# Storing the latents' z once as float32 and cutting it into high and low parts in the perceiver

## The reference, cut to what matters

```python
# z: what the perceiver's queries, keys and values are computed from, per batch
z_x   = layernorm(layernorm(x))  * ln_l_g + ln_l_b     # 512 rows, 512 features
z_ctx = layernorm(ctx)           * ln_x_g + ln_x_b     # 77 rows, 512 features
q     = z_x @ Wq                                       # 16 heads of 64
k, v  = concat(z_ctx, z_x) @ Wkv                      # the kernel keeps z_x first, then z_ctx
out   = softmax(q k^T / 8, masked) v
```

## Time and profile before

| what | value |
|---|---|
| median of 3 runs | 3122.73 us (3119.6 to 3123.52) |
| the profiled execution | 3116.59 us |
| its span, first to last instruction | 3114.8 us |
| PE busy | 2756.6 us, 88% |
| DVE busy | 2101.4 us, 67% |
| ACT busy | 1575.4 us, 51% |
| POOL busy | 1466.0 us, 47% |
| latents stage, by the trace | 923 to 1049 us |
| perceiver stage, by the trace | 1049 to about 2640 us |

### The profile page before, as it was taken

How to read it: one execution, slowest core, us unless ns; L and a number is a source line. 1 busy time by engine, 2 the same in 40 slices (tenths; PEclk the granted TensorE clock), 3 DMA queues, 4 the chain that set the end, 5 groups by cost and what they waited for, 6 DMA issues and landing times. The chain is left out here.

```text
span 3114.8 us, 43373 instructions
## 1 busy us (share of the span) xinstructions
PE 2756.6 (88%) x15650; PEld 2323.5 (75%) x15650; DVE 2101.4 (67%) x4249; ACT 1575.4 (51%) x3064; POOL 1466.0 (47%) x1087
## 2 busy tenths in 40 slices
PE   6788889986868499999999999999999998689687
PEld 5677777765434389898898988989889897577476
DVE  4766666661338577777777877777777777457655
ACT  2333333321104467676776767767677676101175
POOL 2454444331001155555555555556555565356555
PEclk9899999996975699999999999999999999789899
DMA  5111111114018732323223232233322311857474
GB/s 180 50 49 53 53 53 53 39 35 169 1 50 323 282 70 69 97 70 111 66 69 97 76 105 66 69 100 79 99 68 67 97 51 44 290 203 242 176 263 169
DMA packets 184000, 335.11 MB, mean 108 GB/s; under 512 B 52008, under 2 KB 58155, under 8 KB 176749
## 3 DMA queue, kind: packets, MB, share of 16 engines
q1 hardware_dynamic: 161553, 257.30, 27.9%
q0 software_dynamic: 11680, 45.02, 3.9%
q10 hardware_dynamic: 10560, 30.08, 2.5%
HBM read 164.30 MB, written 146.61 MB: 100 GB/s over the span
## 5 line engine op out<-in xcount | busy, mean ns | idle before, releaser
L1671 POOL TENSOR_SCALAR pa_Pr<-pa_Pr,pa_rs 128x590 f32<-128x590 f32 x512 | 904.1, 1770 | 671.9 <-DVE pa_rs L1898 671.8
L1902 DVE TENSOR_REDUCE pa_least<-pa_S 128x1 f32<-128x590 f32 x512 | 390.5, 763 | 186.3 <-PE pa_S L1735 184.3
L1827 ACT ACTIVATE pa_Pr<-pa_S,pa_least 128x590 f32<-128x590 f32 x512 | 385.8, 753 | 110.0 <-DVE pa_least L1902 105.3
L1852 DVE TENSOR_TENSOR pa_PTl<-pa_W,pa_PTh 128x512 fp32r<-128x512 f32 (+1 forms) x640 | 414.9, 681 | 11.1 <-ACT pa_PTh L1796 8.0
L1796 ACT ACTIVATE pa_PTh<-pa_W 128x512 fp32r<-128x512 f32 (+1 forms) x640 | 366.8, 596 | 96.4 <-PE pa_W L1746 82.2
L1746 PE MATMUL pa_W<-pa_ident,pa_Pr 128*128 128x128 f32 (+1 forms) x2560 | 367.5, 274 | 7.2 <-DVE pa_PTl L1852 5.8
L1746 PEld LDWEIGHTS pa_W<-pa_ident,pa_Pr 128*128 128x128 f32 (+1 forms) x2560 | 302.2, 142 | 37.4 <-DVE pa_PTl L1852 11.8
L1760 PE MATMUL pa_O<-pa_PTh,pa_V 128*128 128x512 f32 (+1 forms) x640 | 288.6, 451 | 16.2 <-DVE pa_PTl L1852 12.2
L1761 PE MATMUL pa_O<-pa_PTl,pa_V 128*128 128x512 f32 (+1 forms) x640 | 252.5, 394 | 0.0
L1733 PE MATMUL pa_S<-pa_U,pa_Qh 128*128 128x296 f32 (+1 forms) x1024 | 228.0, 304 | 7.7 <-DMA pa_Um<-pa_U 7.4
L1735 PE MATMUL pa_S<-pa_Um,pa_Ql 128*128 128x296 f32 (+1 forms) x1024 | 223.4, 300 | 0.0
(11 more groups left out here) (470 smaller groups left out, 6808.1 us busy)
## 6 DMA issues: line engine op xcount, KB each, us to landing
xs_s<-pa_Ql SPq DMA_DIRECT2D x57, 576.0 KB
pa_Um<-pa_U SPq DMA_DIRECT2D x128, 147.5 KB
pa_Qh<-pa_Qh SPq DMA_DIRECT2D x128, 128.0 KB
o_s<-pa_O_hi SPq DMA_DIRECT2D x64, 256.0 KB, 2.0
o_s<-pa_O_lo SPq DMA_DIRECT2D x64, 256.0 KB, 2.3
ex_o_hi<-o_s SPq DMA_DIRECT2D x7, 2048.0 KB, 11.0
ex_o_lo<-o_s SPq DMA_DIRECT2D x7, 2048.0 KB, 16.1
z_s<-la_z_hi ACTq DMA_DIRECT2D x8, 1180.0 KB, 7.3
```

What stands on the lines that cost most here:

```text
L1671: pool.tensor_scalar(p, p, rs[:, g % 2, t:t + 1], None, ALU.mult).then_inc(*pool_s.mark("probs", n))
L1827: act.activation(Pr[g % 2][:, t, :], scored[n % 2], ACT.Exp, scale=-1.0, bias=least[:, g % 2, t:t + 1], accum_out=rs[:, g % 2, t:t + 1]).t ...
L1852: dve.tensor_tensor(out, src, f32(hi_ap), ALU.subtract).then_inc(*dve_s.mark(*name))
L1902: dve.tensor_reduce(least[:, g % 2, t:t + 1], scored[n % 2], AX, ALU.min).then_inc(*dve_s.mark("least", n))
```

## The change

z is stored once, as float32, and cut after it is loaded. In the latents, L1419, L1421, L1474 and L1423 and the tiles z_hi and z_lo go; `full` is stored by one transfer. In the perceiver, `load(b)` brings one transfer of 1180 KB into z[1]. ScalarE copies each chunk of it into z[0] (the high part), and VectorE replaces the chunk in z[1] by its difference from z[0] (the low part). For batch 0 this stands between the cuts of weights 1 and 2. For a later batch chunks 0 and 1 are cut in tick 64b-9 and chunks 2 and 3 in tick 64b-8: on ScalarE behind the exponential of the tick and ahead of its copies of transposes, on VectorE at the end of the tick. The first query product waits chunk by chunk for the low part. As z[1] is now written by the load while z[0] is written later, `load(b)` waits for the old batch's last key and last value product.

```diff
 build_latents, scalar:
-                    act.wait_ge(*dve_s.before(i, "lo", m, C - 1))
+                    act.wait_ge(z_out[m], i * 16 + 16)
                     ...
-                    act.wait_ge(z_out[m], i * 32 + 32)
-                    for c in range(C):
-                        act.wait_ge(*act_s.at(i, "full", m, C, c))
-                        act.activation(z_hi[m][:, c, :], full[m][:, c, :], ACT.Copy).then_inc(*act_s.mark("hi", m, c))
-                    act.wait_ge(*act_s.at(i, "hi", m, C - 1))
-                    act.dma_start(one(z_s[0])..., f32(z_hi[m][:, :, :])).then_inc(z_out[m], 16)
-                    act.wait_ge(*dve_s.at(i, "lo", m, C - 1))
-                    act.dma_start(one(z_s[1])..., f32(z_lo[m][:, :, :])).then_inc(z_out[m], 16)
+                    act.wait_ge(*act_s.at(i, "full", m, C, C - 1))
+                    act.dma_start(one(z_s)..., full[m][:, :, :]).then_inc(z_out[m], 16)
 build_latents, vector:
-                    for c in range(C):
-                        dve.wait_ge(*act_s.at(i, "hi", m, c))
-                        dve.tensor_tensor(z_lo[m][:, c, :], full[m][:, c, :], f32(z_hi[m][:, c, :]), ALU.subtract)
 build_perceiver:
+        z_at = {}
+        for b in range(1, B):
+            tick = LEAD * (b * BP - 1) - 1
+            z_at[tick], z_at[tick + 1] = [(b, 0), (b, 1)], [(b, 2), (b, 3)]
 sync:
             def load(b):
-                for n in range(2):
-                    sp.dma_start(f32(z[n][:, :, :]), z_s[n][b:b + 1]...).then_inc(z_in, 16)
+                if b > 0:
+                    sp.wait_ge(*pe_s.after("K", b * BP - 1, 1))
+                    sp.wait_ge(*pe_s.after(*v_unit(b * BQ - 1, NC - 1)))
+                sp.dma_start(f32(z[1][:, :, :]), z_s[b:b + 1]...).then_inc(z_in, 16)
 tensor, query(p):
-                if p % BP == 0:
-                    pe.wait_ge(z_in, 32 * (p // BP + 1))
                 for k in range(C):
+                    if p % BP == 0:
+                        pe.wait_ge(*dve_s.after("z lo", p // BP, k))
 scalar:
+            def z_hi(b, c):
+                if c == 0:
+                    act.wait_ge(z_in, 16 * (b + 1))
+                act.activation(z[0][:, c, :], f32(z[1][:, c, :]), ACT.Copy).then_inc(*act_s.mark("z hi", b, c))
-            w_scalar(act, 0, FIRST)
+            w_scalar(act, 0, 2)
+            for c in range(C):
+                z_hi(0, c)
+            w_scalar(act, 2, FIRST)
             ...
                 for u in evacuated(n - 1):
                     read(u)
+                for b, c in z_at.get(n, []):
+                    z_hi(b, c)
 vector:
+            def z_lo(b, c):
+                dve.wait_ge(*act_s.after("z hi", b, c))
+                lo(z[1][:, c, :], f32(z[1][:, c, :]), z[0][:, c, :], "z lo", b, c)
-            w_vector(dve, 0, FIRST)
+            w_vector(dve, 0, 2)
+            for c in range(C):
+                z_lo(0, c)
+            w_vector(dve, 2, FIRST)
             ...
                 for u in evacuated(n - 1):
                     if u[0] == "K" and u[2] == 1:
                         read(u)
+                for b, c in z_at.get(n, []):
+                    z_lo(b, c)
```

More of the change, by code:

```diff
@@ L1248, in build_latents @@
     SK = a["ctx_1024"].shape[1]
-    Z = z_s[0].shape[3]
+    Z = z_s.shape[3]
     C, NT = D // P, T // P
@@ L1266, in build_latents @@
         full = two("full", [P, C, Z])
-        z_hi, z_lo = two("z_hi", [P, C, Z], F32R), two("z_lo", [P, C, Z], F32R)
         bank = [st.ps(f"bank{n}", [P, 512]) for n in range(8)]
@@ L1396, in _ @@
                 act.sem_inc(x2_out[m], 16)
-                act.sem_inc(z_out[m], 32)
+                act.sem_inc(z_out[m], 16)
             act.wait_ge(small, 16 * len(smalls))
@@ L1415, in _ @@
                            .then_inc(*act_s.mark("full", m, C, c))
-                    act.wait_ge(z_out[m], i * 32 + 32)
-                    for c in range(C):
-                        act.wait_ge(*act_s.at(i, "full", m, C, c))
-                        act.activation(z_hi[m][:, c, :], full[m][:, c, :], ACT.Copy).then_inc(*act_s.mark("hi", m, c))
-                    act.wait_ge(*act_s.at(i, "hi", m, C - 1))
-                    act.dma_start(one(z_s[0]).rearrange("b p c z -> p (b c) z"), f32(z_hi[m][:, :, :])).then_inc(z_out[m], 16)
-                    act.wait_ge(*dve_s.at(i, "lo", m, C - 1))
-                    act.dma_start(one(z_s[1]).rearrange("b p c z -> p (b c) z"), f32(z_lo[m][:, :, :])).then_inc(z_out[m], 16)
+                    act.wait_ge(*act_s.at(i, "full", m, C, C - 1))
+                    act.dma_start(one(z_s).rearrange("b p c z -> p (b c) z"), full[m][:, :, :]).then_inc(z_out[m], 16)
             for m in range(2):
                 act.wait_ge(x2_out[m], 16 * (PAIRS + 1))
-                act.wait_ge(z_out[m], 32 * (PAIRS + 1))
+                act.wait_ge(z_out[m], 16 * (PAIRS + 1))
         @block.vector
@@ L1471, in _ @@
                     add_and_measure(i, 1 - m)
-                    for c in range(C):
-                        dve.wait_ge(*act_s.at(i, "hi", m, c))
-                        dve.tensor_tensor(z_lo[m][:, c, :], full[m][:, c, :], f32(z_hi[m][:, c, :]), ALU.subtract)\
-                           .then_inc(*dve_s.mark("lo", m, c))
 def build_perceiver(nc, orders, a, z_s, o_s, xs_s, mask_s):
-    B = z_s[0].shape[0]
-    C, Z = z_s[0].shape[2], z_s[0].shape[3]
+    B = z_s.shape[0]
+    C, Z = z_s.shape[2], z_s.shape[3]
     INNER = a["L1_xattn_Wq"].shape[1]
@@ L1592, in load @@
             def load(b):
-                for n in range(2):
-                    sp.dma_start(f32(z[n][:, :, :]), z_s[n][b:b + 1].rearrange("b p c z -> p (b c) z")).then_inc(z_in, 16)
+                if b > 0:
+                    sp.wait_ge(*pe_s.after("K", b * BP - 1, 1))
+                    sp.wait_ge(*pe_s.after(*v_unit(b * BQ - 1, NC - 1)))
+                sp.dma_start(f32(z[1][:, :, :]), z_s[b:b + 1].rearrange("b p c z -> p (b c) z")).then_inc(z_in, 16)
             w_sync(sp, 0, 2)
@@ L1635, in _ @@
                 if p % BP == BP - 1 and p + 1 < PAIRS:
-                    sp.wait_ge(*pe_s.after("K", p, 1))
                     load(p // BP + 1)
@@ L2650, in two_layers @@
     si_s, vo_s = scratch("si_s", B, NS, D), scratch("vo_s", B, NS, D)
-    z_s = [scratch(f"z{n}_s", B, P, D // P, Z) for n in range(2)]
+    z_s = scratch("z_s", B, P, D // P, Z)
     o_s = [scratch(f"o{n}_s", B, INNER // P, P, T) for n in range(2)]
```

## The result

| what | before | after |
|---|---|---|
| median of 10 runs each | 3121.15 us (3117.72 to 3125.85) | 3134.01 us (3127.23 to 3142.91) |
| ratio, 95% interval | | 1.0043 (1.003 to 1.0056) |
| the profiled execution | 3116.59 us | 3139.5 us |
| its span | 3114.8 us | 3137.7 us |

The account below looks back on a forecast made before the run. TensorE was taken to bound the perceiver; in the latents three resources were near their limit. Terms -7.7 - 4.6 - 2.0 + 15.4 + 13.3 = +14.4 us put the median at 3137 us, range 3127 to 3147.

Parts of the forecast that it names:

- Latents, the batches: Seven latents batches: without cuts and one store, each falls from 12.1 to 11.0 us, -7.7 us in all.
- Latents, the end: End of the latents: the only store can start earlier, so the next stage begins sooner, -4.6 us.
- Perceiver, the start: Perceiver's start: weight 2's load has 1180 KB less ahead of it, so TensorE begins earlier, -2.0 us.
- The waits at the seven changes: Perceiver's changes of batch: landing and cut delay TensorE's first query product by 2.2 us each, +15.4 us.
- The clock there: Same seven changes: a 3.3 us TensorE gap drops the clock to 1.2 GHz, 1.9 us each, +13.3 us.
- The clock that stays up: Rival at the changes of batch: no clock fall, sum only +1.1 us, 3124 us; chance 0.18.
- The cut hides: Rival: z lands by ScalarE's wait in tick 55, a change costs 1.0 us, total 3115 us; chance 0.09.
- The latents did not keep their 12 us: Rival in the latents: half-clock TensorE holds batches at 12 us, so only their end gains, 3145 us; chance 0.07.
- z_lo beside a GpSimd multiply: Rival at changes of batch: z_lo waits for a 1.76 us GpSimd multiply each time, +12 us, 3149; chance 0.06.
- The load's duration: Load of z at a change of batch: 5.7 us from the trace, used in the sum; the skill's estimate 4.8 us.

Follow-up runs that it names:

- gap_filled: Changed kernel plus 12 unread matrix products in TensorE's gap at each change of batch: 3111.58 us, ratio 1.0023 to the kernel before.
- changed_again: The changed kernel measured once more with no further edit: 3133.52 us, ratio 1.0057 to the kernel before.
- chunk_load: Changed kernel with z loaded by four transfers, one per chunk with its own semaphore, cuts in place: ratio 0.9975 to the kernel before.
- latents_keep_cut: Changed kernel whose latents still form the unused high and low parts but store only float32 z: run once, 11.61 us a latents batch.
- latents_alone: Changed latents with the earlier perceiver, which loads the one stored z twice, uncut: 3094.26 against 3105.08 us for the kernel before, ratio 0.9974.
- cut_in_56: Changed kernel with all four chunks cut in tick 56 instead of two in 55: ratio 0.9973 to the kernel before; again 3108.51 us, 0.9969.
- tiny_cut: Changed kernel cutting only two columns of each chunk from batch 1 on, every wait kept, values wrong: ratio 0.9972 to the kernel before.
- cut_in_56_57: Changed kernel with every cut one tick later, chunks 0 and 1 in tick 56, 2 and 3 in 57: ratio 0.9988 to the kernel before.
- cut_in_54_55: Changed kernel with every cut one tick earlier, chunks 0 and 1 in tick 54, 2 and 3 in 55: ratio 1.0137 to the kernel before.

## Why the prediction was right, and where its terms were off

The forecast, slower at 3137 us, was right: measured 3134.0, which is 12.9 above the kernel before where the forecast had 14.3. The mechanism held as described: the order of the engines' work at the change of batch and the fall of the clock behind it, both seen step by step in the trace. That the sum came so near (+14.2 in the trace, +14.4 forecast) is partly luck, since terms were off both ways: the batches gained 4.0 us more than forecast, the stage's end 2.7 us less, and the perceiver lost 1.0 us more. By its steps:

- **Latents, the batches**, -7.7 forecast, -11.7 measured. A term mis-sized: the chain through GpSimd gives 10.43 us a batch, which is the bound I had worked out as 10.5. I moved up to 11.0 because TensorE at the half clock needed 10.6 us. It did not hold the batches: its busy time fell with them, to 9.5 and 7.7 us in the windows shown at the half clock, so the 10.6 us of the earlier trace rows was no need. What stretched it there was not tried.
- **Latents, the end**, -4.6 forecast, -1.9 in the traced execution of after. In the nine other kernels traced that have both the store and the cuts gone, this stretch takes 11.2 to 11.6 us in seven (about -6.0) and 14.9 and 13.6 in two. The last x2 products took the rest in the traced one, through a late load and the half clock; in the two others they took 7.19 us as well. My bound had named an x2 store, not the products.
- **Perceiver, the start**, -2.0 forecast, -1.9 measured: 19.7 us to the first query product in place of 21.6. The cuts of batch 0 lay under the load of weight 2, as forecast.
- **The waits at the seven changes**, +15.4 forecast, +15.8 with the gap filled, one fall of the clock included. There the query is 1.7 to 2.2 us later than before at six changes (2.2 forecast) and 4.6 us at the seventh, so the closeness of the sum owes something to that last one. The parts hold at the first change: landing 5.95 us (5.7), from there to the weighing 3.67 us (3.78), the gap of TensorE 3.54 us (3.3), ScalarE's wait 1.45 us (1.2). The query came after 13.15 us, not 11.6, mostly because the 2.13 us from the weighing to it took 3.53 us at the half clock: that belongs to the next term. One thing I had not seen: at the seventh change the load lands only after 7.9 us and ScalarE waits 3.46 us. This last load took 7.5 to 8.4 us in eight of the fourteen kernels traced and 5.4 to 6.3 in the other six; the cause is open.
- **The clock there**, +13.3 forecast, +13.9 as the difference between `gap_filled` and after, but 8 to 14 us over the five traces of this perceiver and 6 to 11 by the ratios, so the term was rather too large for a usual execution. It fell at all seven in the traced execution, for 6.8 us six times, longer than the 3.6 us I took from the stage's start; the price, 2.4 us a change between a batch of 198.1 and one of 195.7, is between my 1.9 and my bound of 2.8; where the clock was down for 3.4 us, as half of the times in `changed_again`, it is 1.2 us (`chunk_load`). The mechanism read from the latents' windows carried over.
- **The rivals.** The clock that stays up is refuted but for single changes. "The cut hides" did not happen here, and needs only its place moved by one tick; its premise that a gap of 2.1 us leaves the clock up was unsafe, since gaps of 1.8 to 2.0 us had it fall at six of 17 places. The latents did not keep their 12 us. z_lo beside a GpSimd multiply was not seen: at the change of batch L1857 takes 0.73 us a chunk while GpSimd is between two multiplies. The rule of the Trainium skill (SBUF — State Buffer, Who interferes with whom) has no more than its small part: GpSimd's operations L1339 and L1345 took 0.19 and 1.20 us once no low parts ran beside them, and 0.63 and 1.57 us in `latents_keep_cut`, where they do. The page gives a direction and no price for this pair; here it is about 1.2 us over the three operations of each batch (0.44 + 0.41 + 0.37).
- **The load's duration.** The trace's 5.7 us served well (5.4 to 6.0 at the first six changes). The estimate by the Trainium skill (DMA: Bandwidth & Descriptors, Anatomy of one DMA), 4.8 us, was too short for this load: in no kernel traced did such a load land in under 5.2 us.

What stays open: the trace puts the latents' gain, with their end and the start, at 15 to 20 us, the ratios of `latents_alone` and `cut_in_56` at 8 to 11 us, with intervals of 4 us on either side. The two halves measured alone add up to +24 us (1.0102 and 0.9974), the whole to +13 and +18. So some 6 to 10 us of the gain seen in single traced executions are not in the medians. The latents' end, which varies by 4 us, and the experts' stage, by 19 us, are of the right size; no run separates them.

## What to carry to other kernels

An operation moved into engines with in-order queues costs what stands behind its wait, not what it takes: list what is queued behind it on each engine and who waits for that, and look one step later for a place where its data has already landed; here one tick was worth 25 us. Where a new wait leaves TensorE idle for some microseconds, price the clock as well: it made up a quarter to a half of the loss, and shortening the gap to under 2 us recovered most of both. When two resources are near their limits, removing the load of one shows little (0.4 to 0.5 us of 12.1 here), so judge a removal by what bounds next.

## What the runs showed of the hardware

- Idle gaps of TensorE at the changes of batch, and what the granted clock did, over all kernels traced: gaps up to 1.7 us left it at 1.00; of 17 gaps of 1.8 to 2.0 us (`tiny_cut`, `chunk_load`, `cut_in_56_57`) six had it fall; of 34 gaps of 2.8 to 3.9 us, 31; all ten gaps of over 4 us.
- After such a fall the clock was at 1.2 GHz for 3.4 us (19 times) or 6.8 us (25 times), and in `cut_in_54_55`, with gaps of 6.8 and 8.9 us, for 10.2 us twice and 13.7 once. In all 25 cases of 6.8 us it fell before the gap ended, in 18 of the 19 cases of 3.4 us when TensorE was already at work again.
- In the latents the clock is below 1.00 for most of the time although TensorE is busy for most of a batch: 0.53 on average over a batch of 10.50 us with 9.46 us busy, 0.69 over the seven batches; the perceiver keeps 1.00 at 187.5 of 192.
- One transfer of 1180 KB from SP's queue at a change of batch lands in 5.2 to 6.3 us, but in 7.5 to 8.4 us at the last change in eight of the fourteen kernels. In four transfers of 295 KB the first lands after 3.0 to 3.7 us and the last after 5.7 to 6.8.
- z_hi takes 683 ns and z_lo 768 ns a chunk in the perceiver against 708 and 762 in the latents: the cut takes the same in both stages within 4%.
